# A long convolution added to x: who adds, who masks, and who reads the accumulator banks

## The reference

```python
# x: (B=32, H=64, L=1024); length, adapter_ids: (32,)
mask = arange(L) < length[:, None]
u_m = x * mask[:, None, :]
K = 2 * real(einsum('hn,hnl->hl', Cs, exp(dtA[:, :, None] * arange(L))))   # (H, L)
y = irfft(rfft(u_m, 2L) * rfft(K, 2L))[..., :L]      # causal convolution along L
y = y + u_m * D[:, None]
x = x + y * mask[:, None, :]
x = x + einsum('bsi,boi->bso', x, weight[adapter_ids])   # weight: (8, 1024, 1024)
```

## Time and profile before

| | |
|---|---|
| median of 3 runs | 370.63 us (370.62 to 373.22) |
| profiled execution, its own time | 371.04 us |
| its span, first to last instruction | 369.1 us |
| TensorE matmul busy | 314.2 us, 85% |
| VectorE busy | 217.2 us, 59% |
| ScalarE busy | 152.0 us, 41% |
| GpSimd busy | 118.5 us, 32% |
| DMA moved | 81.54 MB, mean 221 GB/s |

### The profile page before, as it was taken

How to read it: one execution, slowest core, us unless ns; L and a number is a source line. 1 busy time by engine, 2 the same in 40 slices (tenths; PEclk the granted TensorE clock), 3 DMA queues, 4 the chain that set the end, 5 groups by cost and what they waited for, 6 DMA issues and landing times.

```text
span 369.1 us, 8266 instructions
## 1 busy us (share of the span) xinstructions
PE 314.2 (85%) x2584; PEld 274.7 (74%) x2585; DVE 217.2 (59%) x361; ACT 152.0 (41%) x210; POOL 118.5 (32%) x133
## 2 busy tenths in 40 slices
PE   0055887399779869899799999999999999999993
PEld 0055787399669869899688888888888888888882
DVE  5977797658866862778722962375222592186200
ACT  1947666132615250142622642655112762174200
POOL 4022048328646492357201810370000430170000
PEclk9998699699969987999999999999999999999999
DMA  7974966999698979996028513921225904842222
GB/s 254 392 292 159 353 231 233 344 419 412 253 375 275 362 277 417 385 411 253 0 59 325 187 30 83 401 86 28 57 57 174 380 14 114 330 181 57 58 59 57
DMA packets 20550, 81.54 MB, mean 221 GB/s; under 512 B 4464, under 2 KB 4656, under 8 KB 16944
## 3 DMA queue, kind: packets, MB, share of 16 engines
q1 hardware_dynamic: 18272, 80.98, 59.3%
q10 hardware_dynamic: 2256, 0.30, 0.5%
HBM read 72.58 MB, written 18.64 MB: 247 GB/s over the span
## 4 chain that ended last, share of the span: by engine, by line
PE 50%; POOL 2%; DVE 1%; issue 1%; ACT 0%; DVEq 0%; ACTq 0%
PE bank L1141 50%; POOL z L473 2%; DVE mid L814 0%; DVE z_lo L990 0%; DVE z L1040 0%; DVE o_tile L1022 0%; ACT z_hi L640 0%; DVEq L990 0%; DVEq L1021 0%; ACTq L640 0%; DVEq L812 0%; ACTq L633 0%; ACTq L685 0%
## 5 line engine op out<-in xcount | busy, mean ns | idle before, releaser
L1080 PE MATMUL bank<-x,strips 128*128 (+6 forms) x1536 | 110.4, 235 | 15.8 <-DMA strips<-k_padded 14.4
L1080 PEld LDWEIGHTS bank<-x,strips 128*128 128x128 f16 x1536 | 104.6, 102 | 21.4 <-issue 15.6
L1141 PE MATMUL bank<-w_hi,z_hi 128*128 128x512 f32 x272 | 83.9, 389 | 2.0 <-DVE z_lo L990 2.0
L1141 PE MATMUL bank<-w_hi,z_lo 128*128 128x512 f32 x272 | 83.8, 389 | 0.0
L1141 PE MATMUL bank<-w_lo,z_hi 128*128 128x512 f32 x272 | 83.7, 389 | 0.0
L492 POOL TENSOR_TENSOR w_raw<-w_raw,ident 128x128 f32<-128x128 f32 x36 | 38.5, 1091 | 117.3 <-DMA w_raw<-in_w 110.3
L473 POOL TENSOR_TENSOR z<-z,mid 128x512 f32 (+1 forms) x31 | 53.9, 1748 | 52.5 <-DVE mid L814 52.4
L1141 PEld LDWEIGHTS bank<-w_hi,z_hi 128*128 128x128 f32 x272 | 51.0, 188 | 13.0 <-issue 2.4
L1141 PEld LDWEIGHTS bank<-w_hi,z_lo 128*128 128x128 f32 x272 | 51.0, 188 | 10.6
L1141 PEld LDWEIGHTS bank<-w_lo,z_hi 128*128 128x128 f32 x272 | 51.1, 188 | 10.6
L990 DVE TENSOR_TENSOR z_lo<-z,z_hi 128x512 fp32r<-128x512 f32 (+2 forms) x36 | 36.1, 1045 | 37.2 <-ACT z_hi L640 37.2
(11 more groups left out here) (166 smaller groups left out, 191.4 us busy)
## 6 DMA issues: line engine op xcount, KB each, us to landing
strips<-k_padded SPq DMA_DIRECT2D x64, 512.0 KB, 8.6
w_raw<-in_w SPq DMA_DIRECT2D x18, 1024.0 KB, 8.5
k_padded<-k_row SPq DMA_DIRECT2D x8, 1152.0 KB, 6.3
out<-o_tile SPq DMA_DIRECT2D x34, 256.0 KB
z<-in_x SPq DMA_DIRECT2D x8, 1024.0 KB, 5.4
w_raw_early<-in_w SPq DMA_DIRECT2D x2, 1024.0 KB, 10.1
k_row<-k_tile ACTq DMA_DIRECT2D x8, 32.0 KB, 6.8
small<-in_params SPq DMA_DIRECT2D x1, 192.0 KB, 2.4
```

Of the source, the lines that this page charges most:

```text
L1080: last = mm(conv_ps[k][:, e * COL + d * B:(e + 1) * COL], strips16[:, k, e, k_part, d, :], x16[:, bass.ds(g % 2, 1), x_part, col:col + (NB ...
L1141: last = mm(slot_ps[par][half][:, :], left_[:, par, c, :], right[:, c, half * HALF:(half + 1) * HALF], start=(c == 0 and left_ is z_hi and ...
```

## The change

- D + 1 takes the place of D (VectorE, one more operation in the first stretch), so that the convolution's result already holds x.
- ScalarE multiplies each half of a bank in place with its scale (`unscale`): two instructions of 128x256 for each pair, 64 in all. They stand at fixed places in ScalarE's order.
- VectorE copies the whole bank over z where the mask is set (`merge_pair`): one predicated copy of 128x512 for each pair, 32 in all, in the places where `mask_pair` stood. Where the mask is not set, z keeps x.
- GpSimd's `add_masked` and VectorE's add of the last pair go, as does `mid`; the zeros come from a tile `blank`.
- TensorE waits for `merged` instead of `masked`. VectorE's hardware loop over turns 2 to 4 is written out.

```diff
+            blank = tile(early, "blank", [P, P])
+            tile(early, "rest_of_blank", [P, 4 * COL - P])
@@ GpSimd
-            def add_masked(g, pairs=range(NPAIR)):
-                pool.wait_ge(x_loaded, g + 1)
-                for k in pairs:
-                    n = g * NPAIR + k
-                    pool.wait_ge(masked, 2 * (n + 1))
-                    nc.gpsimd.tensor_tensor(z_pair[...], z_pair[...], mid[...], ALU.add).then_inc(added, 1)
-            add_masked(0, [0, 1, 2])
-            with pool.Fori(1, NG - 2) as g:
-                left_factor(g + 2)
-                add_masked(g - 1, [3])
-                add_masked(g, [0, 1, 2])
-            add_masked(NG - 3, [3])
+            with pool.Fori(3, NG) as g:
+                left_factor(g)
...
+            add_identity(0)
@@ ScalarE
+            def unscale(g, *pairs):
+                for k in pairs:
+                    n = g * NPAIR + k
+                    act.wait_ge(conv_done, n + 1)
+                    act.wait_ge(x_scale_ready, g + 1)
+                    for e in range(2):
+                        half = conv_ps[k][:, e * COL:(e + 1) * COL]
+                        nc.scalar.activation(half, half, ACT.Copy, scale=xk_inverse[:, bass.ds(2 * n + e, 1)]
+                                             ).then_inc(unscaled, 1)
...
             x_high(1)
+            unscale(0, 0)
             sum_x(2)
             sines(3)
+            unscale(0, 1)
             k_high(2)
             store_k(2)
+            unscale(0, 2)
             exchange(3)
+            unscale(0, 3)
             x_high(2)
             sum_x(3)
+            unscale(1, 0, 1)
             k_high(3)
             store_k(3)
+            unscale(1, 2)
             with act.Fori(4, NG) as g:
                 sines(g)
+                unscale(g - 3, 3)
                 x_high(g - 1)
+                unscale(g - 2, 0)
                 exchange(g)
+                unscale(g - 2, 1)
                 sum_x(g)
                 k_high(g)
                 store_k(g)
+                unscale(g - 2, 2)
+            unscale(NG - 3, 3)
             x_high(NG - 1)
+            unscale(NG - 2, 0, 1)
...
-            split_high(0, [0, 1])
+            split_high(0, [0])
+            unscale(NG - 2, 2, 3)
+            split_high(0, [1])
+            unscale(NG - 1, 0, 1)
             act.wait_ge(table_ready, 1)
...
-            act.wait_ge(added, (NG - 1) * NPAIR)
-            act.wait_ge(conv_done, (NG - 1) * NPAIR + 2)
+            act.wait_ge(merged, (NG - 1) * NPAIR)
             high_parts(first_slot, 0, slice(0, H - GH), early_hi_ready)
-            act.wait_ge(added, NG * NPAIR - 1)
-            act.wait_ge(added_last, 1)
+            unscale(NG - 1, 2, 3)
+            act.wait_ge(merged, NG * NPAIR)
             high_parts(first_slot, 0, slice(H - GH, H), z_hi_ready)
@@ VectorE
+            chain.mark(v.tensor_scalar(d_row, d_row, 1.0, None, ALU.add))
...
-            def mask_pair(g, k):
-                n = g * NPAIR + k
-                dve.wait_ge(conv_done, n + 1)
-                if not (isinstance(n, int) and n < 2):
-                    dve.wait_ge(added, n - 1)
-                dve.wait_ge(x_scale_ready, g + 1)
-                for e in range(2):
-                    v.scalar_tensor_tensor(mid[:, k % 2, e, :], conv_ps[k][:, e * COL:(e + 1) * COL],
-                                           xk_inverse[:, bass.ds(2 * n + e, 1)],
-                                           mask[:, :, :].rearrange("p c b -> p (c b)"),
-                                           ALU.mult, ALU.mult).then_inc(masked, 1)
+            def merge_pair(g, k):
+                n = g * NPAIR + k
+                dve.wait_ge(unscaled, 2 * (n + 1))
+                dve.wait_ge(x_loaded, g + 1)
+                v.copy_predicated(z_pair[:, n, :, :],
+                                  mask[:, :, :].rearrange("p c b -> p (c b)").bitcast(i32).unsqueeze(1).to_broadcast([P, 2, COL]),
+                                  conv_ps[k][:, :].rearrange("p (e n) -> p e n", e=2)).then_inc(merged, 1)
...
-                mask_pair(g - 1, NPAIR - 1)
-                mask_pair(g, 0)
+                merge_pair(g - 1, NPAIR - 1)
+                merge_pair(g, 0)
                 x_low(g + 1)
                 k_scaled_out(g + 2)
-                mask_pair(g, 1)
+                merge_pair(g, 1)
                 k_low(g + 2)
...
-            with dve.Fori(2, NG - 3) as g:
+            for g in range(2, NG - 3):
                 turn(g)
...
-            last_pair = z_pair[:, H // 2 - 1, :, :].rearrange("p e n -> p (e n)")
-            v.tensor_tensor(last_pair, last_pair, mid[...], ALU.add).then_inc(added_last, 1)
@@ TensorE
-                    pe.wait_ge(masked, 2 * ((g - 1) * NPAIR + k + 1))
+                    pe.wait_ge(merged, (g - 1) * NPAIR + k + 1)
...
-            pe.wait_ge(masked, 2 * NG * NPAIR)
+            pe.wait_ge(merged, NG * NPAIR)
```

More of the change, by code:

```diff
@@ L131, in ssm_conv_then_adapter_kernel @@
             strips = tile(early, "strips", [P, NPAIR, 2, L])
-            mid = tile(early, "mid", [P, 2, 2, COL])
+            blank = tile(early, "blank", [P, P])
+            tile(early, "rest_of_blank", [P, 4 * COL - P])
             small = tile(early, "small", [P, 38 * H])
@@ L262, in ssm_conv_then_adapter_kernel @@
         conv_done = sem("conv_done")
-        masked = sem("masked")
-        added, added_last = sem("added"), sem("added_last")
+        unscaled, merged = sem("unscaled"), sem("merged")
         early_hi_ready, early_lo_ready = sem("early_hi_ready"), sem("early_lo_ready")
@@ L466, in left_factor @@
                 nc.gpsimd.tensor_tensor(left[:, :, :], left[:, :, :], swapped[:, :, :], ALU.add).then_inc(left_ready, 1)
-            def add_masked(g, pairs=range(NPAIR)):
-                pool.wait_ge(x_loaded, g + 1)
-                for k in pairs:
-                    n = g * NPAIR + k
-                    pool.wait_ge(masked, 2 * (n + 1))
-                    nc.gpsimd.tensor_tensor(z_pair[:, bass.ds(n, 1)].rearrange("p o e n -> p (o e n)"),
-                                            z_pair[:, bass.ds(n, 1)].rearrange("p o e n -> p (o e n)"),
-                                            mid[:, k % 2, :, :].rearrange("p e n -> p (e n)"), ALU.add).then_inc(added, 1)
             left_factor(0)
@@ L584, in x_high @@
                                      scale=x_scale[:, bass.ds(g, 1)]).then_inc(x_hi_ready, 1)
+            def unscale(g, *pairs):
[7 more added lines that the diff above has]
+                                             ).then_inc(unscaled, 1)
             sines(0)
             act.wait_ge(zeros_ready, 1)
-            act.dma_start(k_row[:, 0:P], mid[0:H, 0, 0, 0:P]
+            act.dma_start(k_row[:, 0:P], blank[0:H, :]
                           ).then_inc(zeros_stored, 16)
@@ L721, in reduce_angle @@
                 last(v.tensor_scalar(r, r, *limits, ALU.max, ALU.min))
-            v.memset(mid[0:H, 0, 0, 0:P], 0.0).then_inc(zeros_ready, 1)
+            v.memset(blank[0:H, :], 0.0).then_inc(zeros_ready, 1)
             dve.wait_ge(params_loaded, 16)
             expm1_parts(exponent, 2 * H)
+            chain.mark(v.tensor_scalar(d_row, d_row, 1.0, None, ALU.add))
             link(v.scalar_tensor_tensor(expd, expm, 1.0, scale2f, ALU.add, ALU.mult))
@@ L910, in turn @@
                 x_scales(g + 2)
-                mask_pair(g, 2)
-            mask_pair(0, 0)
+                merge_pair(g, 2)
+            merge_pair(0, 0)
             angles(3)
             x_low(1)
-            mask_pair(0, 1)
+            merge_pair(0, 1)
             k_scaled_out(2)
             k_low(2)
-            mask_pair(0, 2)
+            merge_pair(0, 2)
             factors(3)
@@ L928, in _ @@
             v.tensor_reduce(least_adapter, ids[0:1, 0:B], AX, ALU.min).then_inc(least_ready, 1)
-            with dve.Fori(2, NG - 3) as g:
+            for g in range(2, NG - 3):
                 turn(g)
             turn(NG - 3)
-            mask_pair(NG - 3, NPAIR - 1)
+            merge_pair(NG - 3, NPAIR - 1)
             x_low(NG - 1)
@@ L950, in _ @@
             v.tensor_copy(values[:, 2:3], own).then_inc(slots_placed, 1)
-            mask_pair(NG - 2, 0)
-            mask_pair(NG - 2, 1)
+            merge_pair(NG - 2, 0)
+            merge_pair(NG - 2, 1)
             dve.wait_ge(table_rows, 1)
@@ L1022, in finish_last @@
                 v.tensor_copy(o_tile[:, par, HALF:L], slot_ps[par][1][:, :]).then_inc(out_dve, 1)
-            mask_pair(NG - 2, 2)
+            merge_pair(NG - 2, 2)
             split_low(0, 0)
-            mask_pair(NG - 2, 3)
+            merge_pair(NG - 2, 3)
             split_low(0, 1)
-            mask_pair(NG - 1, 0)
-            mask_pair(NG - 1, 1)
+            merge_pair(NG - 1, 0)
+            merge_pair(NG - 1, 1)
             first_slot = [field(dve, 0, f, B - 1) for f in (F_B0, F_B1)]
@@ L1034, in _ @@
             low_parts(first_slot, 0, slice(0, H - GH), early_lo_ready)
```

(5 more changed lines are left out.)

## The result

The changed kernel takes 378.11 us (median of 4 runs, 377.33 to 379.66), the kernel before 371.05 beside it: ratio 1.0177, 95% interval 1.0132 to 1.0222. It is slower by about 7 us (7.1 by the medians, 6.6 by the ratio, which is not the quotient of the two medians).

A forecast was written before the change was run, and what follows sets the result against it. The end moves with the start of slot 0's first matmul, ahead of 816 unbroken matmuls. Terms 3.85 + 2.2 - 0.5 - 1.3 + 0.15 = +4.4 us, added to the 370.63 median, gave 375.0 us; range 370.4 to 379.0.

The forecast's parts named there:

- slower still: Rival, chance 0.10: the low clock comes in turns 2 and 4 too, two more slow pairs, +4.4, 379.4 us.
- Prices: New operations: ScalarE's unscale 0.45 us each, 0.85 a pair (bounds 0.67 to 1.17); VectorE's merge 0.69 (0.55 to 1.11).
- The turn: Turns 2 to 5: exchange queued behind unscale, x_low holds GpSimd's line 463, so TensorE waits 2.5 us for left each turn.
- c+5.6: Time when GpSimd's left is ready, 5.6 us after c, the end of convolution (g,0); TensorE finishes (g,1) at c+3.1.
- Store of group 3: Store of K rows moves from 66.93 to about 73, copy from 74.58 to about 80, strips just in time for (2,2).
- Where turn 2 began: Turn 2 on TensorE: (2,0) ends at 82.4, rows of K at 88.0, (2,2) at 88.7 instead of 86.1: +2.6.
- The later turns: Start of third convolution pair: (3,2) +1.7, (4,2) +3.0, (5,2) +2.4; (6,2) +3.85 by late strips, slow pair +2.2.
- Hidden anyway: Rival, chance 0.28: late rows of K are absorbed because stores land behind queued strips; +1.2, near 371.8 us.
- the ring: Loop of rows of K, store, copy, strips, convolution, next rows but one; whatever delays the rows of K comes back.
- Faster: Rival, chance 0.15: lines 463 and 466 get in ahead of x_low, left at c+3.3, about 366 us.
- Tail: From the end of the last convolution to the first slot matmul: 3.5 us instead of 4.8, -1.3.
- The small operation for D + 1: One more operation in VectorE's first stretch, where all others wait for VectorE: +0.15 us (bounds 0 and 0.3).

The follow-up runs named there:

- the repeat: The changed kernel once more, unchanged, on the chip of three other experiments: 378.42 us against 372.22, ratio 1.0138.
- e2: Changed kernel with VectorE's x_low(g+1) moved ahead of merge(g, 0) in every turn: 370.72 us against 371.99 for the kernel before, ratio 0.9934.
- e8: Changed kernel with x_low(g+1) ahead of merge(g, 0) in turns 2 to 5 only: 374.35 us against 372.22 for the kernel before, ratio 1.0070.
- e1: Changed kernel with exchange(g) ahead of unscale(g-2, 0) in ScalarE's loop: 373.75 us against 371.99 for the kernel before, ratio 1.0042.
- e6: Changed kernel with exchange ahead of unscale on ScalarE and x_low ahead of merge on VectorE, all turns: 371.56 us against 372.22, ratio 0.9937.
- e7: Changed kernel with x_low(2) ahead of merge(1, 0) in turn 1 only: 375.92 us against 372.22 for the kernel before, ratio 1.0112.
- e9: Changed kernel with exchange ahead of unscale on ScalarE, and x_low(2) ahead of merge(1, 0) in turn 1 only: 371.55 us against 372.13, ratio 0.9993.
- e4: Changed kernel with small matmuls filling TensorE's waits, 14 in turns 1 to 5 and 28 ahead of (6,2): 374.48 us against 371.99, ratio 1.0071.
- e11: Changed kernel with shorter fillings of small matmuls, 9 in turns 1 to 5 and 20 ahead of (6,2): 372.46 us against 372.13, ratio 1.0009.
- e10: e9 with small matmuls, 8 behind the rows of K in turns 1 to 5 and 14 ahead of (6,2): 370.72 us against 372.13, ratio 0.9951.
- e3: Kernel before with one more wait: ScalarE's exchange waits for the end of convolution (g-2, 0). 374.15 us against 371.99, ratio 1.0031.

## Why the prediction was right, and where its sum was off

The direction, the place and the mechanism held; the size was +7.1 us by the medians of 4 runs (6.6 by the ratio; 6.2 and 5.1 in the repeat), where I had 4.4. The 378.11 us lie 0.9 below the upper end of the range, and that end had been set for the rival "slower still". That the range held it owes something to luck.

**Prices.** Unscale 0.442 us each (taken 0.45), the pair 0.81 from start to end (0.85). The estimate from the Trainium skill (ScalarE: Activation LUTs, "What ACT_TABLE_LOAD costs"), 0.89, lay further off. Merge 0.735 (0.69). The bounds were far wider than was needed. Half of the four masks in 1.66 us is 0.83; the 0.87 in my text is what two take elsewhere in that trace. Masks and last add together fell by 5.5 us, where I had some 6.

**The turn.** `left` at c+5.6, a wait of 2.5: measured 5.3 in turn 3 (c = 100.7, end 106.0), 2.33 in each of turns 2 to 5. That the collision with `x_low` decides is shown by e2 and e8, where it was taken away and the order on ScalarE kept.

**Store of group 3** "to about 73", its copy to about 80, "just in time" for (2,2): 72.45 and 81.09, 71.21 and 78.33 in the repeat, and (2,2) had no wait for strips in either. (My sum there, 80 and 8.9, is 88.9 and not 88.6.) What I missed is that it would be next in line: e1 and e8 put `left` in time and then wait for strips at (2,2).

**Where turn 2 began.** I let turn 2 begin from an unshifted (1,2). In the profile (1,2) started at 72.70 instead of 71.08, 73.01 in the repeat, so (2,2) came 3.8 us later and not 2.6. That is 1.6 us outside my sum. Nothing shows that the change made it. The store of group 2 did come about 1 us later (57.3 to 58.8 against 56.8 to 57.2), behind merges and unscales of group 0. But in e1, e2, e6, e7, e8 and e9, whose code is the same up to there, (1,2) started at 69.5 to 70.8, ahead of the kernel before. Between this store and its copy lay 3.8 to 8.5 us from one profiled execution to the next. Why it was late in both executions of the changed kernel stays open.

**The later turns.** (3,2) +3.9 (I had +1.7), (4,2) +5.0 (+3.0), (5,2) +5.8 (+2.4), (6,2) +9.2 (+3.85). The term that was sized wrong is the clock: I let only (3,2), as before, and (6,2) be slow, and spared (5,2). In fact all five pairs were slow, together 9.1 us over 3.22 each, in the kernel before 4.8 in the same turns. I had this as the rival "slower still", with 0.10, for turns 2 and 4. It was the case itself: e4 and e11 show the pairs at 3.2 and 2.5 to 4 and 5 to 6 us less. The evidence that I weighed, idle of 1.25 us without effect and of 3 us with it, left 2.3 us open, and I took the mild side. A second part is the way from the store of group 7 to (6,2): 17.4 us in both executions of the changed kernel, 15.2 before, where I had moved one with the other. In the profiles without a filling ahead of (6,2) it is 15.2 to 17.6; what sets it was not looked into.

**Hidden anyway.** The store of group 4 was 2.6 us later than before (91.75) and its copy 3.9 later (99.45): nothing was absorbed. Once `left` was in time (e9, e10), though, the strips set the pace, so the ring does swallow gains. **Faster** did not occur: line 463 got in ahead of `x_low` in no turn.

**Tail.** -1.3 forecast, -1.7 measured. The small operation for D + 1 (+0.15) was not tried alone. The first store was at 26.81 to 27.25 in the kernels with it and at 26.91 to 27.09 in those without, so no cost is to be seen.

**Still open.** How the loss divides between lateness and clock, since each wait does both, and the experiments overlap. The interval of each ratio is 0.3 to 0.6% wide to either side, and a difference of two ratios is less certain still.

## What to carry to other kernels

Before a step is put into an engine's list, look what stands behind it there, and which engine's lock, store or copy that is waiting for: here 58 us less work on GpSimd and 15 less on VectorE cost 7 us, because a small copy was queued behind a wait and so came to lie beside a long VectorE operation. When several steps of a ring are late, one experiment for each can find little: taken away alone, the two latenesses gave 0.7 to 1.1% and 0.3 to 0.7%, together 2.0 to 2.4%. Short waits of TensorE have a second price in the clock of the work behind them; small matmuls on an unused bank in such waits took 1.1% off the kernel before, more than the best order of the change gained (0.7%), though the intervals overlap. And an experiment that wins back the whole loss needs its control in the kernel before, or it names the wrong cause.

## What the runs showed of the hardware

- An in-place scaling in an accumulator bank by ScalarE, 128x256 with a per-partition scale: 442 ns, two in 0.81 us. A predicated copy of 128x512 from a bank into SBUF by VectorE: 735 ns, against 688 for a plain copy.
- A GpSimd 128x256 operation of 0.62 us took 2.46 in all four turns in which a VectorE operation of 2.34 us with two SBUF inputs had started 0.36 us ahead of it. In the experiment with both edits the VectorE operation had started 1.00 us ahead, and it was 1.83. Both times the GpSimd operation ended 0.48 us after the VectorE one. In seven of the eight turns of e8 and e2 it was asked for in the last 0.3 to 0.5 us of the VectorE operation, took 0.78 to 0.95, and ended 0.47 to 0.48 us after it.
- After 2.33 us of idle and the small matmuls of the rows of K, the granted clock was at its lower level for part of the next 4.5 to 5.5 us (means 0.57 to 0.70), in all four turns and in both profiled executions of the changed kernel. After 1.66 us of idle between the rows of K and (4,2) in e1 it was so too (4.85 us, mean 0.64). After 1.47 us of idle ahead of the rows of K (e3, turns 2 and 4) the pairs took 3.22 us at 1.00.
- A store of 32 KB on ScalarE's queue let its copy go 5.7 to 8.7 us later for groups 1 to 7 in the two executions of the changed kernel (72.45 to 81.09 for group 3). For group 0, before any strips were queued, it was 1.7 us in the kernel before and in one execution of the changed kernel, 4.1 in the other.
- A VectorE instruction of 128x512 from float32 to int32 took 0.48 to 0.49 us three times and then 0.83 to 1.39 in the kernel before, and 0.49 in all eight places of the changed kernel, where GpSimd's adds are gone.
